# New instruction orders in four phases, transpositions set behind runs of small tiles, and 21 extra products at the start of a two-layer attention and expert kernel

## The reference

```python
x = x + attention(norm(x), ctx; 16 heads of 8, Wq, bq, Wk, bk, Wv, bv, Wo, bo)   # L0, keys 64 per sequence
x = x + sum_e w[n,e] * (relu(norm(x) @ W1[e] + b1[e]) @ W2[e] + b2[e])           # L0, 8 experts, top 2 by a gate
x = x + attention(norm(x), ctx; 16 heads, Wq, Wk, Wv, Wd)                        # L1
# L1 cell, sequential over the tiles: two steps of 64 rows in each of the 64 tiles
f, i = sigmoid(xt @ wf.T + c @ uf.T + bf), sigmoid(xt @ wi.T + c @ ui.T + bi)
c = f * c + i * tanh(xt @ wc.T + c @ uc.T + bc)
out = x + tanh(norm(x) @ wo.T + c_final @ uo.T + bo)
```

## Time and profile before

| what | value |
|---|---|
| median of three runs | 842.12 us |
| the profiled execution | 841.05 us, of which the span of instructions 839.2 us |
| PE busy | 820.6 us (98%) |
| DVE busy, ACT busy | 775.3 us (92%), 775.4 us (92%) |
| POOL busy | 682.5 us (81%) |
| mean granted TensorE clock | 0.992 |

### The profile page before, as it was taken

One profiled execution on the slowest core, in us unless ns is written; L12 is line 12 of the kernel. 1 busy time (PEld: TensorE's weight loads), 2 busy tenths in 40 slices (PEclk: granted clock), 3 DMA queues, 4 the chain that ended last, 5 costly groups with the idle time before them and its releaser, 6 DMA issues.

```text
span 839.2 us, 42592 instructions
## 1 busy us (share of the span) xinstructions
PE 820.6 (98%) x15268; PEld 743.5 (89%) x15268; DVE 775.3 (92%) x2778; ACT 775.4 (92%) x2490; POOL 682.5 (81%) x1292
## 2 busy tenths in 40 slices
PE   8899999999999999999999999999999999999996
PEld 5688999999999999999999999999999999998884
DVE  6789999999999999999999999999999999999855
ACT  5899999999999999999999999999999999998874
POOL 5888998888888888888888888888888888887644
PEclk7999999999999999999999999999999999999999
DMA  9400000000000000000000000000000000000005
GB/s 345 175 3 3 2 4 4 4 3 4 3 3 4 4 4 3 4 3 4 3 4 4 4 4 4 3 3 4 3 4 3 4 3 4 4 4 3 3 3 201
DMA packets 6969, 17.74 MB, mean 21 GB/s; under 512 B 752, under 2 KB 2288, under 8 KB 6768
## 3 DMA queue, kind: packets, MB, share of 16 engines
q1 hardware_dynamic: 6336, 14.36, 4.5%
q10 hardware_dynamic: 432, 0.68, 0.3%
HBM read 10.84 MB, written 4.19 MB: 18 GB/s over the span
## 4 chain that ended last, share of the span: by engine, by line
PE 90%; DVE 4%; ACT 3%; issue 2%; POOL 1%; DVEq 0%; POOLq 0%; ACTq 0%
PE ps L458 15%; PE ps L480 13%; PE ps L393 13%; PE ps L378 8%; PE ps L423 7%; PE ps L554 6%; PE ps L540 5%; PE ps L329 4%; PE ps L358 4%; PE ps L437 3%; PE ps L343 3%; PE ps L320 2%; PE ps L404 2%; PE ps L321 2%; PE ps L493 1%
## 5 line engine op out<-in xcount | busy, mean ns | idle before, releaser
L1512 POOL TENSOR_TENSOR h<-Ex 128x512 f32<-128x512 f32 (+1 forms) x144 | 165.9, 1152 | 57.6 <-issue 51.2
L1106 DVE TENSOR_REDUCE mx<-ps 128x8 f32<-128x512 f32 (+1 forms) x288 | 167.0, 620 | 8.2 <-PE ps L378 7.9
L1120 DVE TENSOR_TENSOR Ex<-ps,mx 128x512 f32<-128x512 f32 (+1 forms) x288 | 170.8, 617 | 0.1
L819 ACT ACTIVATE ET<-ps 128x512 f32<-128x512 f32 (+1 forms) x288 | 166.0, 584 | 3.2 <-PE ps L393 2.9
L808 ACT ACTIVATE Ex<-Ex 128x512 f32<-128x512 f32 (+1 forms) x288 | 165.1, 608 | 2.0 <-DVE Ex L1120 1.8
L393 PE MATMUL ps<-w,Ex 128*128 128x128 f32 x1024 | 158.8, 275 | 0.1
L1212 DVE SCALAR_TENSOR_TENSOR acc<-ps,we,acc 128x128 f32<-128x128 f32 x448 | 147.9, 330 | 1.3 <-issue 0.2
L458 PEld LDWEIGHTS ps<-xT,w 128*128 128x128 f32 x1024 | 124.2, 191 | 24.6 <-issue 24.6
L458 PE MATMUL ps<-xT,w 128*128 128x128 f32 x1024 | 144.9, 284 | 0.0
L857 ACT ACTIVATE hT<-ps,w 128x128 f32<-128x128 f32 x512 | 140.1, 398 | 3.1 <-PE ps L458 2.8
L480 PE MATMUL ps<-w,hT 128*128 128x128 f32 x1024 | 139.0, 279 | 0.0
(11 more groups left out here) (108 smaller groups left out, 1847.4 us busy)
## 6 DMA issues: line engine op xcount, KB each, us to landing
cx<-ctx_dram SPq DMA_DIRECT2D x7, 512.0 KB, 12.5
x<-x_dram SPq DMA_DIRECT2D x7, 512.0 KB, 13.1
out_dram<-x SPq DMA_DIRECT2D x14, 256.0 KB, 2.7
w<-weights_dram SPq DMA_DIRECT2D x2, 512.0 KB, 5.4
w<-weights_dram SPq DMA_DIRECT2D x1, 576.0 KB, 8.7
out_dram<-x SPq DMA_DIRECT2D x4, 128.0 KB, 2.6
w<-weights_dram ACTq DMA_DIRECT2D x1, 328.0 KB, 4.4
w<-weights_dram ACTq DMA_DIRECT2D x1, 256.0 KB, 3.1
```

The costliest lines, as they stand in the source:

```text
L819: e.activation(ET[:, j % 2, r, lo:hi, :, :], b[:, 256 * lo:256 * hi].rearrange("p (c w q) -> p c w q", c=hi - lo, w=2), ACT.Copy).then_inc ...
L1106: e.tensor_reduce(mx[:, j % 2, r, 4 * lo:4 * hi], b[:, 256 * lo:256 * hi].rearrange("p (j k) -> p j k", k=64), AX.X, ALU.max).then_inc(sig ...
L1120: e.tensor_tensor(Ex[:, j % 2, r, 256 * lo:256 * hi].rearrange("p (j k) -> p j k", k=64), b[:, 256 * lo:256 * hi].rearrange("p (j k) -> p ...
L1512: e.tensor_tensor(u, v[:, :, :, 0:32], v[:, :, :, 32:64], ALU.add).then_inc(sig("half1"), 1)
```

## The change

`STARTS` becomes (-1, 6, 12, 66): four phases with new lists for every engine, and new `LAG` and `AHEAD`. `EVEN` goes from 2 to 7. The banks follow from the new `USES` by the same rule. A table `BUSY` adds 21 float32 products of two resident weights at eight places; each set is issued behind the stage's bank wait and ahead of its wait for data. Five VectorE stages get waits on older work of VectorE itself.

```diff
-EVEN = 2
+EVEN = 7
+BUSY = {("turnx", 0): 4, ("q", 0): 1, ("S", 0): 3, ("q", 1): 4, ("S", 1): 2, ("q", 2): 2, ("e2", 0): 4,
+        ("S", 2): 1}
-STARTS = (0, 15, 72)
+STARTS = (-1, 6, 12, 66)
...
+            def keep_busy(b, name, j):
+
+                for _ in range(BUSY.get((name, j), 0)):
+                    e.matmul(b[:, 0:128], wkv[:, WK, :], wkv[:, WK1, :], start=True, stop=True, skip_group_check=True)
...
                 b = bank(i, "turnx")
+                keep_busy(b, "turnx", j)
                 if j == 0:
                     e.wait_ge(sig("in_w1"), 16)
                 e.wait_ge(sig("n"), j + 1)
...
                 b = bank(i, "q")
+                keep_busy(b, "q", j)
                 e.wait_ge(sig("xT"), j + 1)
...
                 b = [bank(i, f"S{r}") for r in range(4)]
+                keep_busy(b[0], "S", j)
                 e.wait_ge(sig("qT"), j + 1)
...
                 b = bank(i, f"e{r}")
+                keep_busy(b, f"e{r}", j)
                 e.wait_ge(sig(f"E{r}"), j + 1)
...
+                if t >= 2:
+                    e.wait_ge(sig("mv"), t - 1)
                 e.bn_stats(st[:, t % 2, 0, :], x[:, t, :]).then_inc(sig("st0"), 1)
...
+                if j >= 2:
+                    e.wait_ge(sig(f"D{r}"), j - 1)
                 e.tensor_reduce(mx[:, j % 2, r, 4 * lo:4 * hi],
```

More of the change, by code:

```diff
@@ L564, in tensor_program @@
                     project_bias()
+                for r in due(i, "y1"):
+                    experts(r, 1)
+                for r in due(i, "e1"):
+                    turn_e(r, 1)
+                for r in due(i, "e3"):
+                    turn_e(r, 3)
+                for r in due(i, "h1"):
+                    hidden(r, 1)
+                for r in due(i, "sB"):
+                    step(r, 1)
+                for r in due(i, "p"):
+                    project(r)
+                for r in due(i, "turnw"):
+                    turn_w(r)
@@ new lines, in tensor_program @@
+                for r in due(i, "wx0"):
+                    out_inputs(r, 0)
+                for r in due(i, "q"):
+                    query(r)
+                for r in due(i, "wx1"):
+                    out_inputs(r, 1)
+                for r in due(i, "gate"):
+                    gate(r)
+                for r in due(i, "sA"):
+                    step(r, 0)
+                for r in due(i, "e2"):
+                    turn_e(r, 2)
+                for r in due(i, "y0"):
+                    experts(r, 0)
@@ new lines, in tensor_program @@
+                for r in due(i, "e0"):
+                    turn_e(r, 0)
+                for r in due(i, "S"):
+                    scores(r)
+                for r in due(i, "turnx"):
+                    turn_x(r)
+                for r in due(i, "xin"):
+                    cell_inputs(r)
+                for r in due(i, "rt"):
+                    turn_r(r)
+                for r in due(i, "kv"):
+                    keys_values(r)
+                for r in due(i, "h0"):
+                    hidden(r, 0)
@@ L593, in tensor_program @@
[L593 to L606, removed]
@@ L1264, in vector_program @@
+                for r in due(i, "mx3"):
+                    maxima(r, 3)
+                for r in due(i, "gidx"):
+                    gate_index(r)
                 for r in due(i, "mx2"):
                     maxima(r, 2)
+                for r in due(i, "sb3"):
+                    differences(r, 3)
+                for r in due(i, "c5"):
+                    combine(r, 5)
+                for r in due(i, "sm"):
+                    sums(r)
+                for r in due(i, "c1"):
+                    combine(r, 1)
@@ new lines, in vector_program @@
+                for r in due(i, "c3"):
+                    combine(r, 3)
+                for r in due(i, "aT"):
+                    normal(r)
+                for r in due(i, "sb2"):
+                    differences(r, 2)
+                for r in due(i, "c6"):
+                    combine(r, 6)
+                for r in due(i, "c7"):
+                    combine(r, 7)
+                for r in due(i, "rc"):
+                    inverse(r)
+                for r in due(i, "st2"):
+                    stats_experts(r)
@@ L1270, in vector_program @@
-                for r in due(i, "sb2"):
-                    differences(r, 2)
+                for r in due(i, "st13"):
+                    stats_attention(r)
+                for r in due(i, "ag"):
+                    spread(r)
+                for r in due(i, "gsc"):
+                    gate(r)
+            for i in range(STARTS[1], STARTS[2]):
                 for r in due(i, "sb3"):
@@ L1285, in vector_program @@
                     combine(r, 2)
+                for r in due(i, "uB"):
+                    update(r, 1)
                 for r in due(i, "rc"):
@@ new lines, in vector_program @@
+                for r in due(i, "gtop"):
+                    gate_top(r)
+                for r in due(i, "st2"):
+                    stats_experts(r)
+                for r in due(i, "st0"):
+                    stats_inputs(r)
+                for r in due(i, "ag"):
+                    spread(r)
+                for r in due(i, "gidx"):
+                    gate_index(r)
+                for r in due(i, "mx0"):
+                    maxima(r, 0)
+                for r in due(i, "mx2"):
+                    maxima(r, 2)
@@ new lines, in vector_program @@
+                for r in due(i, "mx1"):
+                    maxima(r, 1)
+                for r in due(i, "sb0"):
+                    differences(r, 0)
+                for r in due(i, "sb1"):
+                    differences(r, 1)
+                for r in due(i, "sb2"):
+                    differences(r, 2)
+                for r in due(i, "mx3"):
+                    maxima(r, 3)
+                for r in due(i, "c0"):
+                    combine(r, 0)
+            for i in range(STARTS[2], STARTS[3]):
+                for r in due(i, "sb1"):
+                    differences(r, 1)
+                for r in due(i, "sb2"):
+                    differences(r, 2)
+                for r in due(i, "mx3"):
+                    maxima(r, 3)
+                for r in due(i, "aT"):
+                    normal(r)
+                for r in due(i, "c0"):
+                    combine(r, 0)
+                for r in due(i, "sb3"):
+                    differences(r, 3)
+                for r in due(i, "c1"):
+                    combine(r, 1)
+                for r in due(i, "c2"):
+                    combine(r, 2)
+                for r in due(i, "sm"):
+                    sums(r)
+                for r in due(i, "c3"):
+                    combine(r, 3)
+                for r in due(i, "rc"):
+                    inverse(r)
+                for r in due(i, "c4"):
+                    combine(r, 4)
+                for r in due(i, "xa"):
+                    project(r)
+                for r in due(i, "c5"):
+                    combine(r, 5)
@@ L1301, in vector_program @@
                     gate(r)
+                for r in due(i, "uA"):
+                    update(r, 0)
                 for r in due(i, "c7"):
@@ L1412, in vector_program @@
-                for r in due(i, "c4"):
-                    combine(r, 4)
-                for r in due(i, "mx0"):
-                    maxima(r, 0)
-                for r in due(i, "sb2"):
-                    differences(r, 2)
-                for r in due(i, "uA"):
-                    update(r, 0)
-                for r in due(i, "c1"):
-                    combine(r, 1)
-                for r in due(i, "c8"):
-                    combine(r, 8)
-                for r in due(i, "gtop"):
-                    gate_top(r)
```

621 lines of the change are left out of this document (346 added, 275 removed), and 88 rows, old and new, of tables (AHEAD, LAG, USES).

## The result

The changed kernel takes 851.91 us (median of 20 executions, 840.04 to 856.01) against 841.87 us for the kernel before (20 executions, 840.90 to 842.95): 1.0084 of its time, 95% interval 1.0068 to 1.0101. It is slower, and above the range forecast (831 to 847). That ratio leaves out the executions more than 1.5% above the fastest, here presumably those with the most long rounds; the medians alone stand at 1.012. The executions spread over 16 us where those before spread over 2; that spread is part of the answer. The profiled execution has a span of 850.0 us, 10.8 more than before. By the starts of the score groups the start of the program (to `j` = 12, 108.88 us) lost 0.9 us, the 50 rounds of the middle (to `j` = 62, 722.85 us) 8.7 and the end 1.1.

The account below looks back on a forecast made before the run. It took a VectorE–TensorE loop of 12.09 us to bound middle rounds, against 12.10 before. Middle -0.5, start 0 and end 0 gave 840.5 against the profiled 841.05, or 841.6 by the median; it said 841.5 us, range 831 to 847.

Parts of the forecast that it names:

- TensorE's work: Middle round: the new order of transpositions and products saves 0.20 us, so TensorE alone would need 11.90 us instead of 12.10.
- The loop of 12.09 us: Middle round: `e2` to `y1` on TensorE, `c5`, VectorE's list to `sb2`, back to `e2`; ends last, giving back 0.19 us.
- TensorE's part: Middle loop: four transpositions, then `y0` through `y1` until `c5` starts, 4.25 us.
- VectorE's stretch: Middle loop: VectorE's list from `c5` round to `sb2`, 7.78 us, plus 0.06 until the waiting load starts.
- rival 1: Middle: TensorE is the bound after all, the loop being shorter than 11.9 us; 830.5 us, chance 0.22.
- dependent pairs: VectorE's list in the middle: `c5` and `c6` now touch, costing 0.12 to 0.13 us more than with an independent neighbour.
- The worse end of the middle: Upper end of the middle's range: rounds of 12.14 us, given as 2.5 us lost over 52 rounds.
- The wait of `e2` for `sb2`: Middle: TensorE's weight load for `e2` waits for VectorE's `sb2`, near 0.19 us in each round.
- The start: First rounds: added products delay, later rounds of 5.1 us pay back; net 0, from 3 us gained to 4 lost.
- Rival 2: Start: the products are paid and not paid back, the clock stays at half; 846 us, chance 0.26.
- The end: End of the program: lists differ but the cell's chain and stores are the same; 0, with 1.5 us either way.
- The chances: Whole kernel: faster 0.38, same 0.26, slower 0.36; the forecast itself had 0.42.

Follow-up runs that it names:

- rt_after_h1: `pool_late` with TensorE's transposition `rt` of the middle phase put back behind `h1`: undisturbed rounds of 11.93 us, middle 599.7 us.
- loop_long: `pool_late` with four extra `bn_aggr` on VectorE ahead of `mx0`, between `c5` and `sb0`, in every middle round: rounds of 12.11 us, span 844.3 us.
- pool_late: The changed kernel with a one-column memset on GpSimd ahead of its second addition of halves 0, so it starts after `ve`: 836.05 us, 0.9928 of before.
- again5: The changed kernel itself, unaltered, timed on another chip against the kernel before: 839.13 us (7 executions), 0.9974 of before.
- pool_order: The changed kernel with GpSimd's power and product (`pw`) ahead of its halves (`hv0`) in the third phase: 846.7 us, 1.0058 of before.
- ve_one_input: The changed kernel with `nm` and `ve` made by `tensor_scalar`, one SBUF input each instead of two: 836.81 us, 0.9941 of before.
- slack_used: `pool_late` with four extra `bn_aggr` on VectorE between `c1` and `c2`, outside the stretch from `c5` to `sb0`: 832.54 us in one execution, rounds of 11.88.

## Why the prediction was wrong

- **TensorE's work** (12.10 to 11.90): right, 11.88. Each term is there: 0.05 for `rt` (shown by `rt_after_h1`), and in the chain 0.06 for `e2` and 0.11 around the gate.
- **The loop of 12.09 us**: wrong by 0.23. This is the step that put my forecast where no round was. The path was right, `sb2` to `e2` to `y1` to `c5` and round VectorE's list: TensorE's part, from the end of `sb2` to `c5`, takes 4.30 us where I had 4.25 + 0.06. The error is in VectorE's stretch, 7.55 us in a free round against 7.78: I took it from rows in which `nm` and `ve` stood 0.22 us apart, and took 0.08 off for a wait. But that 0.22 was itself a hold. In the kernel before, VectorE's and GpSimd's timelines read

```profile
423.17 0.30 DVE L1095 SCALAR_TENSOR_TENSOR nm<-mv,ones 128x4 f32<-128x4 f32 x1
423.39 0.15 DVE L1096 SCALAR_TENSOR_TENSOR ve<-mv,ones 128x4 f32<-128x4 f32 x1
```

```profile
422.99 0.45 POOL L1526 TENSOR_TENSOR x<-x,w 128x128 f32<-128x128 f32 x1
```

  with `nm` ending 17 to 25 ns after GpSimd's L1526, in 47 of the 50 middle rounds; unheld, the two are 0.08 apart. That is 0.14 us. The rest is 0.05 that I had too much between `gsc` and `uA` and 0.04 ahead of `ag`. So a loop was there, as `loop_long` shows, but at 11.86, and TensorE's 11.88 would have ended last: rival 1, in `pool_late` (836.05) and the others without holds. It named 830.5 us; the start and the disturbed rounds make up the difference. Its reason was not the one I gave: `c5` and `c6` are still 0.39 apart (327.19 and 327.57 us), so dependent pairs do cost. (The prediction calls it the second rival in one place; it is the first. The worse end of the middle, 12.14 us a round, is 2.1 us lost and not 2.5.)
- **The hold** was in no case of mine, and it is the cause of the loss: the step that failed is that I put what VectorE and GpSimd cost each other at nothing, without a reason. A delay of 0.57 us in a loop of 11.86 gives 12.43; 30 such rounds are 16.5 us, and a middle that would have gained 6 lost 9. I had priced waits between queues and the two engines' instructions each by itself. The row that would have told me, a `nm` of 0.30 us beside a `ve` of 0.15 with the same shape, lay in the stretch that I summed.
- **The wait of `e2` for `sb2`** at 0.19 in each round: in free rounds there is none; in the 36 long ones it is there, 0.15 us, behind a wait of `pv` for `sb0` that I had not expected. `c5` waits for `y1` as I wrote.
- **The start**: `S(0)` at 11.25 (I said 11.4), the products behind bank waits as I said, and the clock stayed at full, which I had put at 4 in 10 (nine of eleven profiles with the products, as said above). `S(2)` at 23.0 where I said 22.1. But the three rounds behind it take 5.4 to 6.4 us and not 5.1, so 0.9 us was lost instead of 2.2 gained. Rival 2's mechanism, products paid and not paid back, is right in kind but not in size (it had the clock at half and S(2) behind 24 us): taking them out is worth 2.2 us in one pair and 3.2 in the other, both without the full clock. Rival 2's 846 us is nearest to the 851.9 by luck: it has the middle at 12.10.
- **The end**: 1.1 us, within the 1.5 allowed. Its cause was not looked into.
- **The chances**: with `ve` free in the middle's rounds the change is 0.6 to 0.7% faster (836.81, 836.05, and 835.65 of the kernel itself), with `ve` held in most it is 1.2% slower (851.91), in 43 of the 50 middle rounds, in the two kernels made for it, 2.2 to 2.3% (859.94 and 860.7, one execution each). My forecast lies between, where only executions with some ten held rounds come out; a median like the 839.1 of `again5` would have met my range by luck, with the same step wrong.

What stays open: what makes the start of either engine vary by 10 ns between executions, and why the first 20 executions lost the race so much oftener than the 8 later ones, which ran on two chips; whether the chip has a part in it was not tested. The loop itself favours staying: in the first profile the 30 held rounds of the middle come in three rows (rounds 16 to 26, 36 to 45 and 50 to 61, with rounds 17, 37 and 39 disturbed in another way), and each row follows a round disturbed in another way (15, 35, 49). That a delay in one round sets when the next round's exponentials, and with them GpSimd's addition, are ready would explain it, and is not shown.

## What to carry to other kernels

Before summing a stretch of a timeline, compare each instruction with the shortest of its own shape: one that is longer and ends a fixed few ns after another engine's instruction was probably held by it, and an order that moves the two apart or together moves the time. Look at VectorE's small SBUF operations beside GpSimd's long ones, above all within a loop that has no slack; there, an order or one cheap instruction that sets the two starts well apart keeps the time from hanging on a few ns (here GpSimd's addition starting later did; `pool_order`, which moved it more, cost over 0.2 us a round elsewhere). Work added to fill waits has to be weighed by what stands behind it in the queue, not by the clock that it keeps up.

## What the runs showed of the hardware

- Between `ve` and the addition L1703 the hold turns on 1 to 2 ns of recorded start: with GpSimd ahead by 18 ns or less `ve` took 0.155 us, from 20 ns on 0.73; at 19 both occur, and one unheld case lies at 21. It is no general figure: behind GpSimd's first addition (L1699) `ve` was held with 3 ns (0.74 us at 40.94 us of the first profile), and `nm` with 1 ns (57.12 us of the second).
- It seems to work the other way round too: in the second profile of the changed kernel the additions that began 16 to 19 ns ahead and did not win took up to 0.78 us for their usual 0.74.
- `bn_aggr`, also reading SBUF, was never held (0.18 us at most, with some 180 of the 256 in a profile inside a GpSimd operation); `scalar_tensor_tensor` and, from two columns on, `tensor_scalar` on the aggregates were. Held instructions of both forms end 13 to 28 ns after GpSimd's.
- Two to five rounds of 12.6 us (12.8 in `loop_long`) stand in the profiles whose other rounds take 11.88 to 12.11. VectorE's timeline of `ve_one_input`, round 35:

```profile
383.97 0.38 DVE L1212 BATCH_NORM_AGGREGATE mv<-st 128x2 f32<-128x6 f32 x4 [0.24 <-issue]
384.38 0.57 DVE L1215 TENSOR_SCALAR nm<-mv 128x4 f32<-128x4 f32 x1
```

  A gap of 0.24 us for which the trace has no releaser makes `nm` late, and then it is held by the addition: together 0.7 us. They fall on nearly the same rounds (15, 35 and 37, with 17, 39 or both) in the six profiles of this kind without extra VectorE work, and on others with it (22, 26, 43, 49 in `loop_long`, 22 and 28 in `slack_used`); that the gap is the loading of instructions is a guess from this, not shown.
